# A graph network layer on one core: where TensorE loads its loop counts, and five places for pair one-hots

## What is computed

```python
agg = segment_sum(x[src], dst, num_segments=6250)
h = relu(agg @ W_rel + b_rel + x @ W_root)            # 512 wide
gates = h @ W_ih.T + b_ih + b_hh                       # i, f, g, o
c = sigmoid(i) * tanh(g)
out = layernorm(x + (sigmoid(o) * tanh(c)) @ W_fc + b_fc)
```

## Time and profile before

| what | value |
|---|---|
| median of three runs | 1827.25 us (1826.65 to 1827.99) |
| profiled execution | 1824.41 us, its span 1822.5 us |
| TensorE busy, products | 1513.5 us (83%) |
| VectorE busy | 815.9 us (45%) |
| ScalarE busy | 418.5 us (23%) |
| GpSimd busy | 1281.0 us (70%) |
| mean granted clock of TensorE | 0.910 |
| gathers L400, count and mean | 924, 1043 ns |
| pair products L451 | 640 + 412 |

### The profile page before, as it was taken

The page is one execution under the profiler, slowest core; times in us unless marked ns, Lnnn a source line. Parts: engine busy times, 40 slices in busy tenths (PEclk is TensorE's granted clock), DMA queues, the critical chain, the costliest instruction groups (busy, mean ns, idle before and its releaser), DMA issues.

```text
span 1822.5 us, 31499 instructions
## 1 busy us (share of the span) xinstructions
PE 1513.5 (83%) x6882; PEld 1213.0 (67%) x6883; DVE 815.9 (45%) x1763; ACT 418.5 (23%) x743; POOL 1281.0 (70%) x1926
## 2 busy tenths in 40 slices
PE   0157688697988898788998889899988888999997
PEld 0023355486767676667887667688876676888886
DVE  8877666431322654531324565422244654222332
ACT  0001021110112332220222333212223332222333
POOL 5875877777777877877777668776763668656640
PEclk9976677698988998889999999999998998999999
DMA  9563555576766555567766445576652455766540
GB/s 342 209 233 87 150 161 145 157 225 207 215 195 180 162 162 165 161 198 223 223 206 180 138 133 166 160 246 217 203 155 77 133 146 161 225 189 177 150 122 18
DMA packets 131966, 319.14 MB, mean 175 GB/s; under 512 B 17295, under 2 KB 68268, under 8 KB 130198
## 3 DMA queue, kind: packets, MB, share of 16 engines
q0 software_dynamic: 75264, 245.95, 46.4%
q10 hardware_dynamic: 52632, 54.80, 9.5%
q1 hardware_dynamic: 3936, 16.62, 2.4%
HBM read 298.10 MB, written 19.20 MB: 174 GB/s over the span
## 4 chain that ended last, share of the span: by engine, by line
PE 48%; POOL 21%; issue 19%; DVE 4%; DMA 3%; DVEq 3%; POOLq 1%; ACT 0%; ACTq 0%; SPq 0%
PE ps_blk L537 20%; POOL rows L400 14%; PE ps_agg L476 9%; PE ps_win L464 6%; POOL idx L370 6%; PE ps_y L545 4%; PE ps_blk L519 3%; PE ps_blk L524 3%; PE ps_tr L451 1%; DMA hot_key<-in_xb 1%; POOL rows L385 1%; PE ps_win L451 1%; DMA rows<-x_parts,idx 1%; POOLq L370 1%; DMA wih_sb<-in_x 1%
## 5 line engine op out<-in xcount | busy, mean ns | idle before, releaser
L400 POOL DMA_INDIRECT rows<-x_parts,idx x924 | 963.5, 1043 | 453.5 <-PE ps_agg L476 157.6
L537 PE MATMUL ps_blk<-cell,wih_sb 128*128 128x250 f32 x2400 | 545.5, 385 | 2.9 <-issue 2.2
L537 PEld LDWEIGHTS ps_blk<-cell,wih_sb 128*128 128x128 f32 x2400 | 464.1, 196 | 69.5 <-issue 8.8
L476 PE MATMUL ps_agg<-rows,onehot 128*125 x1112 | 341.8, 462 | 153.2 <-SPq L339 70.8
L476 PEld LDWEIGHTS ps_agg<-rows,onehot 128*125 128x125 f32 x1112 | 234.1, 216 | 227.5 <-issue 175.9
L906 DVE SCALAR_TENSOR_TENSOR onehot<-iota_f,tile_first,dst_u 128x500 f32 (+1 forms) x278 | 207.0, 746 | 291.7 <-PE ps_agg L476 171.6
L370 POOL COPY idx<-src_sb 128x1 int32 x956 | 264.4, 277 | 16.7 <-issue 9.7
L664 ACT ACTIVATE cell<-ps_blk,bg_sb 128x250 f32<-128x250 f32 x300 | 140.8, 470 | 544.0 <-PE ps_blk L537 470.2
L897 DVE TENSOR_TENSOR hot_key<-iota_h,rel 128x980 f16 x263 | 174.4, 663 | 0.4 <-issue 0.4
L464 PE MATMUL ps_win<-adj,hot_key 128*128 128x250 f32 x784 | 170.7, 375 | 2.4 <-DMA hot_key<-in_xb 1.5
L464 PEld LDWEIGHTS ps_win<-adj,hot_key 128*128 128x128 f32 x784 | 148.0, 190 | 21.6 <-DMA hot_key<-in_xb 4.0
(11 more groups left out here) (125 smaller groups left out, 914.2 us busy)
## 6 DMA issues: line engine op xcount, KB each, us to landing
hot_key<-in_xb ACTq DMA_DIRECT2D x28, 896.0 KB
rows<-x_parts,idx POOLq DMA_INDIRECT x924
x_t<-in_xT ACTq DMA_DIRECT2D x25, 250.0 KB
x_n<-in_x ACTq DMA_DIRECT2D x25, 250.0 KB
out<-y ACTq DMA_DIRECT2D x25, 250.0 KB
x_parts<-wih_sb SPq DMA_DIRECT2D x4, 1024.0 KB, 6.8
wih_sb<-in_x ACTq DMA_DIRECT2D x6, 512.0 KB, 9.7
x_parts<-cell SPq DMA_DIRECT2D x2, 1024.0 KB, 7.6
```

The costliest lines, as they stand in the source:

```text
L400: g.indirect_dma_start(rows_f[:, k * QC + j, :], None, x_parts, bass.IndirectOffsetOnAxis(ap=idx[:, k, j:j + 1], axis=0)).then_inc(landed[ ...
L476: ins = mm(o, onehot[:, hot * QC + j, 0:TN], rows[:, ds(slot + j, 1), :].squeeze(1), start=(first and j == 0), stop=False)
L537: last = mm(o, wih_sb[:, k, col:col + P], h_t[:, k, :], start=(k == 0), stop=(k == KH - 1))
```

## The change

Places for pairs go from four to five. TensorE no longer unpacks spans: `table` has a new row of words, one for each window, with the pair counts of both spans. `load_windows` loads them into registers for all windows of a slot; it, and `load_part` for the step count of the next `part_sum`, run inside `gates`, ahead of the second gate's products (in the first turn straight ahead of the windows). VectorE loads the next span's word inside the loop over chunks, between `hot_lo` and `hot_key`. The place is advanced by five operations without a comparison. The source indices are kept as 16-bit words: the 32-bit ones land in the last slot of the ring, VectorE copies them right after `table_ready`, GpSimd waits for that copy (`src_short`), and its gather into that last slot waits until two VectorE operations have read the 32-bit ones (`src_read`).

```diff
-PAIRS = 4
+PAIRS = 5
+        def load_span(engine, regs, at):
+            engine.reg_load(regs[0], table[0:1, at:at + 1] if isinstance(at, int) else table[0:1, ds(at, 1)])
-        def unpack(engine, regs, at):
+        def unpack(engine, regs):
             packed, first, past = regs
-            engine.reg_load(packed, table[0:1, at:at + 1] if isinstance(at, int) else table[0:1, ds(at, 1)])
             engine.reg_alu(first, packed, PACK, ALU.python_divide)
...
-        def next_pair(engine, pair, place, more):
-            engine.reg_add(pair, pair, 1)
+        def next_place(engine, place, past_last):
+            engine.reg_add(past_last, place, 2 - PAIRS)
+            engine.reg_alu(past_last, past_last, 0, ALU.max)
+            engine.reg_alu(past_last, past_last, -PAIRS, ALU.mult)
             engine.reg_add(place, place, 1)
-            engine.reg_alu(more, place, PAIRS, ALU.is_lt)
-            engine.reg_alu(place, place, more, ALU.mult)
+            engine.reg_add(place, place, past_last)
...
-            pool.wait_ge(edges_in, 32)
+            pool.wait_ge(src_short, 1)
...
-                g.tensor_copy(idx[:, k % RING, j:j + 1], src_sb[:, ds(chunk + j, 1)]).then_inc(idx_copied, 1)
+                g.tensor_copy(idx[:, k % RING, j:j + 1], src_u[:, ds(chunk + j, 1)]).then_inc(idx_copied, 1)
...
+                if k == RING - 1:
+                    pool.wait_ge(src_read, 2)
...
+            def load_windows(w0, n_windows):
+                for i in range(n_windows):
+                    at = w0 + (T_WINDOW + i)
+                    even, odd = window_pairs[i]
+                    pe.reg_load(counts_of, table[0:1, at:at + 1] if isinstance(at, int) else table[0:1, ds(at, 1)])
+                    pe.reg_alu(even, counts_of, PACK, ALU.python_divide)
+                    pe.reg_alu(odd, counts_of, PACK, ALU.python_mod)
...
-                        first, past = unpack(pe, pe_regs, at)
-                        with pe.Fori(first, past, QC):
-                            s = pe.snap(pair_0, min_val=0, max_val=MAX_PAIRS)
+                        n = pe.snap(window_pairs[i][side], min_val=1, max_val=STEPS)
+                        s0 = pe.snap(pair_0, min_val=0, max_val=MAX_PAIRS)
+                        with pe.Fori(0, n) as m:
+                            s = pe.snap(m + s0, min_val=0, max_val=MAX_PAIRS)
...
-                            next_pair(pe, pair_0, place, more_places)
+                            next_place(pe, place, past_last)
+                        pe.reg_add(pair_0, pair_0, n)
...
+                    if which == 1 and load_next is not None:
+                        load_next()
...
+                    def load_next():
+                        load_windows(w, wins[j])
+                        if j + 1 < KH and parts[j + 1] is not None:
+                            load_part(t, *parts[j + 1])
...
             dve.sem_inc(table_ready, 1)
+            dve.wait_ge(edges_in, 32)
+            v.tensor_copy(src_u[:, :], src_i).then_inc(src_short, 1)
             split_pieces(POOL_PIECES, PARTS)
...
-                first, past = unpack(dve, dve_regs, at + T_SPAN)
+                first, past = unpack(dve, dve_regs)
...
+                    load_span(dve, dve_regs, at + (T_SPAN + 1))
                     dve.wait_ge(rel_made, s + 1)
...
-                    next_pair(dve, pair_0, place, more_places)
+                    dve.reg_add(pair_0, pair_0, 1)
+                    next_place(dve, place, past_last)
```

More of the change, by code:

```diff
@@ L101 @@
 TURNS = make_turns()
+MOST_WINDOWS = max(max(u.wins) for u in TURNS)
 HEAD = len(TURNS)
@@ L242, in gnn_kernel @@
         edges_in = sem("edges_in")
+        src_short = sem("src_short")
+        src_read = sem("src_read")
         bias_in = sem("bias_in")
@@ L424, in _ @@
             pair_0 = pe.alloc_register("pair_0")
-            pe_regs = [pe.alloc_register(name) for name in ("packed", "first", "past")]
+            more_steps = pe.alloc_register("more_steps")
+            counts_of = pe.alloc_register("counts_of")
+            window_pairs = [[pe.alloc_register(f"window_pairs{i}_{side}") for side in range(2)] for i in range(MOST_WINDOWS)]
             place = pe.alloc_register("place")
-            more_places = pe.alloc_register("more_places")
+            past_last = pe.alloc_register("past_last")
             pe.reg_mov(place, 0)
@@ L479, in visit, with load_part @@
                 ins.then_inc(hot_used, 1)
+            def load_part(t, a, part):
+                at = t + ((T_MORE_A, T_MORE_B)[part] + a)
+                pe.reg_load(more_steps, table[0:1, at:at + 1] if isinstance(at, int) else table[0:1, ds(at, 1)])
             def part_sum(t, a, part):
                 o = ps_agg[a][0:TN, :]
-                col = (T_MORE_A, T_MORE_B)[part] + a
-                more = pe.value_load(table[0:1, t + col:t + col + 1] if isinstance(t, int) else table[0:1, ds(t + col, 1)], min_val=1, max_val=STEPS - 1)
+                more = pe.snap(more_steps, min_val=1, max_val=STEPS - 1)
                 s0 = pe.snap(step_0, min_val=0, max_val=MAX_STEPS)
@@ L525, in hidden_rel, with gates @@
                 last.then_inc(blk_ready, 1)
-            def gates(n, j):
+            def gates(n, j, load_next=None):
                 if j == 0:
@@ L550, in turn @@
                 for j in range(KH):
+                    def load_next():
+                        load_windows(w, wins[j])
+                        if j + 1 < KH and parts[j + 1] is not None:
+                            load_part(t, *parts[j + 1])
                     if parts[j] is not None:
+                        if j == 0 or (j == 1 and parts[0] is None):
+                            load_part(t, *parts[j])
                         part_sum(t, *parts[j])
-                    if not first:
-                        gates(n - 1, j)
+                    if first:
+                        load_next()
+                    else:
+                        gates(n - 1, j, load_next)
                     if wins[j] > 0:
@@ L853, in _ @@
             link(v.tensor_copy(hi, row_i[:, 0:SPANS]))
+            sides = hi.rearrange("p (w s) -> p w s", s=2)
+            v.scalar_tensor_tensor(table[:, T_WINDOW:T_WINDOW + WINDOWS], sides[:, :, 0], float(PACK), sides[:, :, 1], ALU.mult, ALU.add).then_inc(setup, 1)
+            n_setup[0] += 1
+            dve.wait_ge(setup, n_setup[0])
             link(v.scalar_tensor_tensor(hi, hi, float(QC), lo, ALU.mult, ALU.add))
@@ L911, in part_hots @@
                 col = (T_MORE_A, T_MORE_B)[part] + a
-                more = dve.value_load(table[0:1, t + col:t + col + 1] if isinstance(t, int) else table[0:1, ds(t + col, 1)], min_val=1, max_val=STEPS - 1)
+                dve.reg_load(more_steps, table[0:1, t + col:t + col + 1] if isinstance(t, int) else table[0:1, ds(t + col, 1)])
+                more = dve.snap(more_steps, min_val=1, max_val=STEPS - 1)
                 tile = t + a if isinstance(t, int) else dve.snap(t + a, min_val=0, max_val=TILES - 1)
```

24 lines of the change are left out of this document (13 added, 11 removed).

## The result

The changed kernel takes 1767.6 us (median of 4 runs, 1763.9 to 1770.3) against 1827.0 (4 runs, 1825.7 to 1828.0): a ratio of 0.967, 95% interval [0.966, 0.969]. The direction was forecast; the size was not, 59 us against 14, and the time lies outside the range of 1798 to 1835.

A forecast was written before the change was run, and what follows sets the result against it. Setup and first block bound it to 152 us, GpSimd's gathers to 857, TensorE from 860; +1.1 + 8.5 in the head, -3 of GpSimd's waits and -21 behind 860 gave -14.4, so 1813 us, range 1798 to 1835.

The forecast's parts named there:

- TensorE's spans and gates: Pair periods behind 860 us: shorter spans less loads moved into the gates, -21 us, bounds -10 and -32.
- The window loads in the gate block: TensorE's gates: one load, a division and a remainder added per window, 0.62 us, bounds 0.50 and 0.80.
- The openers: Two stops of 5.5 and 5.6 us before step products opening the pair periods, left out of the 46.6 us closable.
- The clock: TensorE's granted clock, 1.00 without pairs and 0.90 with them; regaining it was only a bound of the -21 us.
- The Sequencer Loop: Skill page on queuing during control instructions; by it the moved loads gain nothing and cost VectorE nothing: 1828 us.
- VectorE's load: First block: load paid per pair, pairs 1.63 us apart within a span, first step product at 159.2, +8.5 us.
- Source indices: Head: GpSimd waits for the 16-bit copy, +1.1 us; its 16-bit index copies cost 0, ends -8 and +38 us.
- GpSimd's waits: GpSimd's stage before 857 us: 3 of its 6.0 us of remaining waits for TensorE go, -3 us.
- (1): Rival: the load hides on VectorE, so the head costs only 1 to 2 us: 1805 us; chance 0.12.
- (2): Rival: gates starve, TensorE stops 0.5 to 1.1 us a slot and its clock falls: 1822 to 1828; chance 0.15.
- (3): Rival: VectorE's sequencer becomes the bound of the window turns: 1847 us everywhere, 1836 in half; chance 0.15.
- (4): Rival: the 16-bit index copy is dearer on GpSimd by 0.05 us, +21 us: 1834 us; chance 0.08.

The follow-up runs named there:

- experiment 2: The base with TensorE's loads moved out of the gates, window counts straight ahead of the windows and step counts at the sums' heads: 1828.1 us.
- experiment 3: The base with the same TensorE loads ahead of the first of the three gates instead of the second: 1829.6 us.
- experiment 13: The kernel before the change, with one more product of zeros behind each pair's four: 1807.0 us, ratio [0.987, 0.993].
- the base: The changed kernel with a bounds assertion behind each load of TensorE's pair and step counts and VectorE's step counts: 1775.3 us.
- experiment 9: The base with VectorE's load of the next span ahead of the loop over its pairs, once a span: 1782.3 us.
- experiment 10: The base with VectorE's load of a span's bounds straight ahead of their unpacking, as in the kernel before: 1779.7 us.
- experiment 11: The base with four pair places (1785.3 us), with source indices kept in 32 bits and no 16-bit copy: 1785.6 us.
- experiment 4: The base with each of TensorE's window counts loaded three times in the gate block instead of once: 1873.7 us.
- experiment 5: The base with step counts loaded at the head of each sum again, window counts staying in the gates: 1776.5 us.
- experiment 16: The base with window slots 2, 2, 2, 2 and the gates' loads divided between the second and third gate: 1774.8 us.

## Why the prediction was wrong, step by step

**What bounds it: right in the main.** GpSimd up to 860 us, TensorE's idle behind it, and nearly all of the gain came from there. One turn in GpSimd's stage does not fit: see its waits below.

**TensorE's spans and gates, -21 us: the step that failed.** The two periods measured -52.6. Its terms:
- The spans: predicted -0.55 us each; 1.81 to 1.43 is -0.38. Too large.
- The window loads in the gate block: I charged 0.62 us a window in full, because I counted the sequencer's work as one sum over the slot. But a block of twelve products keeps the sequencer for 1.7 us in which it mostly stands, and 1.1 of the 1.4 us of loads went there. Experiments 2 and 3 show that the place alone, at one load a window, is worth 53 us. With what was put in the prediction, a two-window slot would gain 4 x 0.55 - 2 x 0.62 = 0.96 us (I wrote about 1.1) plus nothing for the part; the slot shown is 11.85 us long (1053.64 to 1065.49). A like slot before ran from 1070.06 to 1083.90, 13.84.
- The openers: I set 11.1 us of idle aside as not closable. 5.3 of them closed, as they did in experiment 13, with the old order of loads. In each of these kernels the sequencer spends 3.5 to 4.4 us in the branch back to the start of the period loop (4.03 and 3.72 us before, 3.62 and 4.39 after); what held the kernel before 2 us longer behind it stays open.
- The clock: it stood among my bounds ("and clock gained back") with no number in the sum. It measures -11.7 us, and -6.8 more come from pair products that overlap once they close up. I had the rows for it, 1.00 against 0.90: 165.5 us of busy time at 0.90 hold 16.6 us lost in that period alone.

So -28.8 us of idle stand where -21 stood, a term too small by 7.8, and three terms that were put at nothing make the rest: -11.7 of clock, -6.8 of overlap, -5.3 of openers.

**The array runs dry behind the first gate: not in this kernel.** I put it at 0.5 us a slot and 1.1 in a slot of three windows. The idle before gates was 2.9 us before and is 3.1 after, in all: the loads took 1.4 us, not 1.7, and the first gate's products last 1.95. In the base, whose loads are longer, it is there, 6.9 and 6.6 us in its two periods.

**The Sequencer Loop.** The prediction weighed Advanced Engine Details and Errata of the Trainium skill, by which other instructions can be read and queued while a control instruction executes, and said that the trace does not agree. For a load that stands between spans this held. Experiments 2 and 3 against the base add that what was issued ahead of a load does run on beside it, while what stands behind the load comes later by it: it is free only in time in which the sequencer would have stood. The page's sentence makes no such distinction.

**VectorE's load, +8.5 us: right in kind, half in size.** Pairs at 1.47 us, not 1.63; the first step product at 155.21, not 159.2: +4.5. Experiments 9 and 10 put the load at 0.2 us a pair, not 0.36, and show that even this does not reach the end.

**Source indices: +1.1 us not found, 0 right.** The first compare of a pair came at 106.03, against 106.28. The index copy rose from 277 to 299 ns, which I had named as a sign of being wrong, and the gather fell from 1050 to 1018; experiment 11 shows that the 16 bits are not behind a gain or a loss.

**GpSimd's waits, -3 us:** 6.0 became 0.9 (25.2 less the one of 24.27), -5.1. That is not the whole of it. The turn whose output product starts at 589.0 us is 4.1 us late against the kernel before (584.9), the next one 3.9 early (642.4 against 646.3). These 8.0 us fell in one turn with windows, of which GpSimd's waits explain 3.0 at most, those between 590 and 660 us; I had put TensorE's saving in this stage at nothing beyond such waits. The turns from there to 976 us take the same time together. By them 3.7 us are gained at 976, where the sum had 1.1 + 8.5 - 3 = 6.6 lost.

**The rivals.** (1) was half true of VectorE: a pair costs 1.47 us, between its 1.17 and my 1.63. (2), starved gates that eat the gain, is what the base begins to show, and what experiments 3 and 4 make of it. (3) never began: VectorE is named before 0.2 us of the pair products' idle. (4) fell.

## What to carry to other kernels

Ask with what lead over the array a sequencer comes to short loops that cost it more than the array: here 3.4 us of issued work, and 2.1 with the loads just ahead of them. Register loads were nearly free ahead of the last eight of twelve products, as long as they were shorter than the 1.95 us of array time issued before them; one assertion more per load was over that and cost 8 us. Once the sequencer's standing time is used up, its work does add up over the slot, and dividing it among the gates gains nothing (experiments 5 and 16). And price idle of TensorE between short groups twice: once as idle, and once as busy time at the lower clock, read from the rows of short stretches behind it.

## What was not expected of the hardware

- Loads ahead of a gate block cost more than their own time: the array stands 2.37 us and then runs 24 products in 6.92 us instead of 5.4, at 0.50 of its clock at first.
- One zero product per pair, 0.39 us of the array each, made the kernel before 1.0% faster, the shorter openers included.
- Three loads of one count instead of one, each with its assertion, cost 98 us. The expectation put the two more at 0.9 us a window; in the pair periods they cost 1.5.
- One more product per pair took the two stops that open the periods from 5.58 and 5.48 us to 2.74 and 2.72. No run says by what.
